# Attention between two feed-forward layers: squares turned by pairs of heads, GpSimd's x parts ahead of the widened sums, projections of the end batches in other steps, a gate product ahead of the last values

## The reference, cut to what matters

```
x = x + 0.5 * ffn(layernorm(x))       # w_gate, w_up 512x2048, w_down; keeps 2 of each 4 hidden members
x = x + attention(layernorm(x))       # 16 heads of 32; ONE key head and ONE value head, shared by all 16
x = x + 0.5 * ffn(layernorm(x))       # the same weights again

def attention(x):
    q = x @ w_q.T ; k, v = split(x @ w_kv.T)
    q, k = rotary(q * s), rotary(k * s)
    p = softmax(where(causal, q @ k.T, -max))
    return (p @ v) @ w_proj.T + b_proj
```

## Time and profile before

| | us |
|---|---|
| median of 3 runs | 2748.62 (2747.45 to 2749.23) |
| the profiled execution | 2747.08 |
| its span | 2745.2 |
| TensorE busy | 2664.2 (97%) |
| VectorE busy | 1860.3 (68%) |
| ScalarE busy | 1105.7 (40%) |
| GpSimd busy | 306.1 (11%) |

### The profile page before, as it was taken

One profiled execution on the slowest core, in us unless ns is written; L12 is line 12 of the kernel. 1 busy time (PEld: TensorE's weight loads), 2 busy tenths in 40 slices (PEclk: granted clock), 3 DMA queues, 4 the chain that ended last, 5 costly groups with the idle time before them and its releaser, 6 DMA issues.

```text
span 2745.2 us, 40751 instructions
## 1 busy us (share of the span) xinstructions
PE 2664.2 (97%) x15008; PEld 2142.6 (78%) x15008; DVE 1860.3 (68%) x3506; ACT 1105.7 (40%) x2368; POOL 306.1 (11%) x318
## 2 busy tenths in 40 slices
PE   8999999999999999899999988999999999999999
PEld 6888888888888887566666667888888888888887
DVE  6667666765675667877777775667666766676655
ACT  4233322333333323777776773333333332333232
POOL 0000000000000004544444420000000000000000
PEclk9999999999999999999999999999999999999999
DMA  4210311121112111544454554211221132103100
GB/s 146 84 46 16 138 46 46 59 96 46 46 62 92 46 46 48 153 110 151 143 152 141 153 169 138 85 46 50 78 80 61 32 106 80 46 16 108 46 15 31
DMA packets 149546, 223.55 MB, mean 81 GB/s; under 512 B 9344, under 2 KB 75136, under 8 KB 149120
## 3 DMA queue, kind: packets, MB, share of 16 engines
q1 hardware_dynamic: 149376, 221.29, 25.2%
HBM read 162.53 MB, written 58.72 MB: 81 GB/s over the span
## 4 chain that ended last, share of the span: by engine, by line
PE 88%; DVE 7%; ACT 2%; issue 1%; POOL 1%; DMA 1%; SPq 0%; DVEq 0%; ACTq 0%; POOLq 0%
PE bank L401 50%; PE bank L422 25%; PE bank L1177 3%; PE bank L1137 3%; PE bank L1114 3%; DVE probs L1405 2%; PE bank L1146 2%; DVE probs L1414 1%; PE bank L284 1%; PE bank L1089 1%; PE bank L1165 1%; ACT probs L1276 1%; POOL xnt_l L1018 0%; ACT pt L1281 0%; DVE qtmp L1391 0%
## 5 line engine op out<-in xcount | busy, mean ns | idle before, releaser
L401 PE MATMUL bank<-xnt_h,wgu_h 128*128 128x512 f32 x2048 | 802.5, 392 | 4.5 <-ACT sg L517 2.8
L401 PE MATMUL bank<-xnt_h,wgu_l 128*128 128x512 f32 x2048 | 798.0, 390 | 0.0
L401 PE MATMUL bank<-xnt_l,wgu_h 128*128 128x512 f32 x2048 | 797.6, 389 | 0.0
L586 DVE TENSOR_TENSOR h<-bank,sg 128x512 f32<-128x512 f32 x256 | 176.8, 691 | 590.9 <-PE bank L401 575.3
L401 PEld LDWEIGHTS bank<-xnt_h,wgu_h 128*128 128x128 f32 x2048 | 384.9, 188 | 85.3 <-ACT sg L517 3.7
L521 ACT ACTIVATE mag<-h 128x512 f32<-128x512 f32 x256 | 162.0, 633 | 713.3 <-DVE h L586 713.3
L401 PEld LDWEIGHTS bank<-xnt_h,wgu_l 128*128 128x128 f32 x2048 | 384.8, 188 | 80.9
L401 PEld LDWEIGHTS bank<-xnt_l,wgu_h 128*128 128x128 f32 x2048 | 385.0, 188 | 78.5
L422 PE MATMUL bank<-wd_h,hs_h 128*128 128x512 f32 x1008 | 392.2, 389 | 0.0
L422 PE MATMUL bank<-wd_h,hs_l 128*128 128x512 f32 x1008 | 392.1, 389 | 0.0
L422 PE MATMUL bank<-wd_l,hs_h 128*128 128x512 f32 x1008 | 392.1, 389 | 0.0
(11 more groups left out here) (134 smaller groups left out, 3118.5 us busy)
## 6 DMA issues: line engine op xcount, KB each, us to landing
raw_gu<-in_w_gu SPq DMA_DIRECT2D x128, 512.0 KB, 5.0
raw_d<-in_w_d SPq DMA_DIRECT2D x128, 256.0 KB, 2.6
squares<-probs SPq DMA_DIRECT2D x128, 256.0 KB, 3.9
pt<-squares SPq DMA_DIRECT2D x32, 1024.0 KB, 5.5
x_mid<-x_sb SPq DMA_DIRECT2D x64, 256.0 KB, 2.7
x_sb<-x_mid SPq DMA_DIRECT2D x10, 1024.0 KB, 5.6
x_sb<-in_x SPq DMA_DIRECT2D x32, 256.0 KB, 4.7
out<-x_sb SPq DMA_DIRECT2D x32, 256.0 KB, 2.1
```

The costliest lines, as they stand in the source:

```text
L401: last = pe.matmul(ps, w[:, r, kind, k], xs[:, b, k], start=(i == 0), stop=(i == 3 * KD - 1))
L586: v.tensor_tensor(h[:, r], bank[UP + r % 2][:, :], sg[:, r % 2], ALU.mult).then_inc(h_done, 1)
```

## The change

1. VectorE turns the squares by pairs of heads (0 and 1, then 2 and 3) and not by halves of the keys. The first pair is turned one step earlier, in the last step of the group before, ahead of the masks of heads 2 and 3 there; it waits for two heads' exponentials. The second pair stays where the second half was, the first instruction of the step is gone.
2. GpSimd's `part_x` moves ahead of `widen` within a step.
3. `TURN_KV` goes from 1 to 2: the keys and values are turned, copied and rotated one step later.
4. The first batch projects in steps 1, 2, 5, 6, 10 (before 0, 1, 5, 9, 10), the last in 2, 6, 10, 14 (before 2, 5, 9, 13).
5. At the end `inside` is called after the gate product and again after the up product of r = 0: the first gate product now comes ahead of the last `weigh`, and the first up product ahead of the output projections.

```diff
@@ gate_up
-                            if inside and r == kind == 0:
+                            if inside and r == 0:
                                 inside()
@@ attention_phase
-            TURN_X, TURN_KV, TURN_K = {11: 0, 12: 1, 13: 2, 14: 3}, 1, 4
+            TURN_X, TURN_KV, TURN_K = {11: 0, 12: 1, 13: 2, 14: 3}, 2, 4
-            FIRST_PROJECT = {0: ("kv", 0), 1: ("q", 0), 5: ("q", 1), 9: ("q", 2), 10: ("q", 3)}
-            LAST_PROJECT = {2: ("out", 0), 5: ("out", 1), 9: ("out", 2), 13: ("out", 3)}
+            FIRST_PROJECT = {1: ("kv", 0), 2: ("q", 0), 5: ("q", 1), 6: ("q", 2), 10: ("q", 3)}
+            LAST_PROJECT = {2: ("out", 0), 6: ("out", 1), 10: ("out", 2), 14: ("out", 3)}
@@ gpsimd step
                         part_output(K // TT - 1)
+                    if nxt + 1 <= BATCHES and k - 1 in TURN_X:
+                        part_x(nxt + 1, TURN_X[k - 1])
                     if k % TT == 2:
                         widen(K // TT)
...
-                    if nxt + 1 <= BATCHES and k - 1 in TURN_X:
-                        part_x(nxt + 1, TURN_X[k - 1])
@@ tensor, behind the last step
+                pe.wait_ge(masked, ALL * HG)
+                yield
                 weigh(ALL // TT - 1)
-                pe.wait_ge(masked, ALL * HG)
                 yield
@@ vector
-                def turn_squares(K, half):
-
-                    v.wait_ge(exp_done, (K + 1) * HG)
-                    n = S // 64
-                    pieces = probs3[:, half * n:(half + 1) * n, :, :].rearrange("p c s n -> p (c s n)")
+                def turn_squares(K, pair):
+
+                    if K >= ALL:
+                        return
+                    v.wait_ge(exp_done, K * HG + 2 * pair + 2)
+                    pieces = probs3[:, :, 2 * pair:2 * pair + 2, :].rearrange("p c s n -> p c (s n)")
                     v.transpose(pieces, pieces).then_inc(squared, 1)
@@ vector step
-                    if i == LONG:
-                        turn_squares(K, 0)
                     mask_scores(K + AHEAD - 1, (0, 1))
                     if i == LONG:
                         turn_squares(K, 1)
                     if 1 in mine:
                         copy_turned(K, 1)
+                    if k % TT == TT - 1:
+                        turn_squares(K + 1, 0)
                     mask_scores(K + AHEAD - 1, (2, 3))
@@ vector, ahead of the first step
+                turn_squares(0, 0)
```

## The result

| | median us | runs | against before |
|---|---|---|---|
| before | 2748.03 | 4 (2745.07 to 2749.23) | |
| after | 2770.99 | 4 (2769.57 to 2773.56) | 1.0086 [1.0069, 1.0104] |
| forecast | 2737.0 (2730 to 2747) | | 0.996 |

The change costs 23 us where I forecast 11.5 us less. The profiled execution took 2771.06 us, its span 2769.3 (2745.2 before).

The account below looks back on a forecast made before the run. Attention was taken as the bound, with TensorE idle 64.0 us and some 23 us lost to the low clock. Batches and end summed to -16.3, new clock falls +4.8: -11.5, so 2737 us, range 2730 to 2747.

Parts of the forecast that it names:

- Step 3: Changes of groups inside a batch: the turn ahead of the masks, with the keys' rotation moved, costs 1.75 us a batch.
- Steps 1 and 2: Batch's end: x part first and earlier turn bring 256-wide scores 1.8 us earlier; clock falls of about 1.5 us go.
- Step 4: First batch, projections moved to later steps: sum -1.3 us, bounds -3 and +3.
- Step 5: Last batch, projections moved and its end-of-batch giving 4.2 us: sum -5.95 us.
- Step 6: The end: the gate product fills TensorE's 3.20 us wait for the load of the squares, -2.8 us.
- A: Clock falls as often, now at all eight first changes of groups and the first batch's step 10: 2746 us, chance 0.18.
- B: Changes of groups: TensorE's chain is late everywhere, all three pay 1.16 us in full: +12.4, 2761 us, chance 0.07.

Follow-up runs that it names:

- e7: Kernel before with x parts ahead of the widened sum, the last batch's new table and the gate product ahead of the last `weigh`: 2724.9 us.
- e1: Kernel after with the keys' rotation back at its old place and the first batch's old table of projections: 2734.4 us.
- e10: Kernel after with GpSimd finishing the first two query tiles only once the keys are widened, and the first batch's old table: 2740.7 us.
- e3: Kernel after with GpSimd finishing the first two query tiles only when VectorE has widened the keys: 2746.8 us.
- e8: Kernel before with GpSimd's last two bias additions delayed to run beside the keys' rotation, no work added: 2766.4 us.
- run 63: Not a follow-up run but a count: VectorE's operations L599 and L602 are each run 63 times in the kernel before, medians 1.22 and 0.69 us.
- e4: Kernel before with only GpSimd's x part ahead of the widened sum: 2725.3 us.
- e11: Kernel before with only the x parts ahead of the widened sum and the gate product ahead of the last `weigh`: 2722.1 us.
- e12: Kernel after with nine unread matmuls of 512 columns ahead of the wait for the widened keys in each batch: 2764.5 us.
- e2: Kernel before with only the keys' turn one step later (TURN_KV 2): 2782.5 us.

## Why the prediction was wrong

From e7 to after each step is one run: 2724.9; the turn by pairs +9.5 (e1); the keys later, with GpSimd kept away, +6.2 (e10); the first batch's table +6.2 (e3); the collision and the clock behind it +24.2 (after).

- **Step 3 failed, in its sentence on the keys.** It took "1.32 us" along to the new place. The step asked which chains on VectorE and TensorE cross there, and not what GpSimd does at that time. GpSimd's four products begin with the first query tile's finish, one step after its projection, and the rotation now stands among them: 3.68 us, and 2.0 more for the clock. That is 4.4 us a batch (75.3 for 70.9), where the whole forecast gain was 11.5. e3 takes it away and gives 24.2 us back; e8 makes it in the kernel before. In before all eight rotations took the same time (0.29, 0.22, 0.22 and 0.29 us for the products and the addition), but its trace did have a price for such a meeting, just ahead of attention, and I didn't look there:

```profile
1060.13 7.53 POOL L1049 TENSOR_TENSOR wq_l<-raw_q,wq_h 128x512 fp32r<-128x512 f32 x4 [0.33 <-ACT wq_h L1330]
...
1060.81 2.31 DVE L599 TENSOR_TENSOR mag<-mag 128x1024 f32<-128x1024 f32 x1
...
1063.15 1.67 DVE L602 TENSOR_TENSOR kept_k<-mag,pmax 128x512 bf16<-128x512 f32 x1
```

The median of L599 is 1.22 us in before and that of L602 0.69; each of the two is run 63 times, and only beside GpSimd's four products did they take 2.31 and 1.67. I gave the rotation's move no bounds at all.
- **The later place of the keys costs something even without the collision.** The step had VectorE's chain 0.4 us shorter by it. From `weigh` at a batch's end over its three changes of groups are 48.67 us in before, 50.42 in e1 (keys early), 51.25 in e3 (keys late, GpSimd kept away). So the 1.75 us are met with the keys at their old place, and at the new one it is 2.6, and 6.2 us over the kernel (e10 against e1). Whether the place or the wait given to GpSimd takes the 0.8 isn't parted. A clean period came to 70.93 us for 70.46, and two falls came, as forecast; e10 has the same waits at that place and three falls, so the exact number is partly luck. The transposes cost what they did.
- **Steps 1 and 2 had the mechanism right.** 1.21 us of wait for 1.25, no fall at the batches' ends, 70.15 us a period in e1. From the third change's `weigh` to the batch's last are 19.67 us in e1 and 21.85 in the one batch of before that had no fall there (1514.62 to 1536.47): 2.2 won for 1.8. They were forecast as equal to the turn's cost, and e4 shows that the two shouldn't have been taken together: the x part alone takes 3.8 us from a period (72.06 to 68.30), and 2.9 between periods without a fall (70.52 to 67.6).
- **Step 4 was mis-sized**, the first batch: -1.3, or +0.5 with the clock, for +8.0; with no collision it is +4.2 (1180.4), and the table's share is 4.5. Its bound of +3 didn't reach it. The clock was low for 23.9 us of the first batch in after and for 17.1 in before, where the forecast had one more fall of 1.8 us.
- **Step 5**: -5.95 for -4.1. The wait of 2.86 us went as forecast; the end of the batch gave 3.2 us (19.93 to 16.77) for 4.2, and the changes of groups before and behind the wait cost 0.8 and 0.9 more than forecast. Of the table alone I expected a gain; next to squares turned at their old place it cost 2.8 us (e7, e11).
- **Step 6**: -2.8 for -2.8.
- **The rivals.** A named the place, the first change of groups in all batches, but as a fall that follows its short waits; with the short waits alone (e3) only two of the middle batches have it. It was the new wait of 2.96 us that brought it to all seven that turn keys; e12, which fills that wait, has it in none of them. B had the sign and half the size, by a mechanism that isn't there: the turns cost 1.9 us a batch, not 3.5. The range ended at 2747, and no case in it was a slower engine.

In e4, e7 and e11 the clock falls at one change of groups, near 1530 us, and at none of those like it before; in e1 at 1540. There VectorE's wait for the store of the squares is the longest up to that place (2.90 us in e4, 2.93 in e7, 3.05 in e11 and 1.89 in e1), and TensorE stands 1.63 and 1.05 us in e4 just there. That the fall follows from these waits was not tried by a run, and why the store landed so late in that batch stays open.

## What to carry to other kernels

Before an operation of VectorE is moved, look up what GpSimd does in the microseconds it moves to, and whether the operation reads two tiles of SBUF: its duration belongs to its place. The price of a meeting may stand elsewhere in the same trace, as an operation whose longest time is far over its median. Move one thing at a time where they can be timed apart: one part of this change (the x parts) was worth 22 us, and the others together took 46 back. A wait of TensorE of 3 us was paid twice here, once itself and once, 2.0 us, in the clock behind it.

## What the runs showed of the hardware

- A VectorE product of two SBUF operands that meets a GpSimd product waits for its end: 0.22 became 1.28 to 1.33 us, 0.29 became 1.23. In after one short product (0.21) passed between two of GpSimd's; in e8 two in a row cost two of GpSimd's.
- The loss is not VectorE's alone. Beside the rotation GpSimd's products took 1.31 us for 1.27, but beside VectorE's longer products at 1060 us of before 1.88 in the mean (7.53 for four), where the like subtraction L1018 took 1.27 at the median.
- A copy from SBUF to SBUF on VectorE (kwide, 128x512) met one too: 1.37 us for 0.43 (e2). Transpositions (one operand, 1.23), masks and products with an operand in a PSUM bank kept their times.
- Nine matmuls that nobody reads, in a wait of 3 us, kept TensorE at 2.4 GHz and made each middle batch 2.0 us shorter.
